# Cross attention: the key tile of 65 keys moves from the eighth to the sixth step of each group

## What is computed

```python
hidden = jnp.concatenate([context, latents], axis=1)      # 1601 + 256 keys
q = (latents @ Wq.T)      # 16 heads of 96
k = (hidden @ Wk.T)       # 4 key heads, each shared by 4 query heads
v = (hidden @ Wv.T)
scores = jnp.einsum('bkgqd,bksd->bkgqs', q, k) * scale
attn = jax.nn.softmax(scores, axis=-1)
out = jnp.einsum('bkgqs,bksd->bkgqd', attn, v)
return out @ Wo.T
```

## Time and profile before

| what | value |
|---|---|
| median of 3 runs | 1926.09 us (1922.92 to 1926.54) |
| profiled execution, its own time | 1923.49 us |
| its span, first to last instruction | 1921.7 us |
| TensorE busy with matmuls | 1871.0 us, 97% |
| VectorE busy | 1233.9 us, 64% |
| ScalarE busy | 1175.2 us, 61% |
| GpSimd busy | 681.4 us, 35% |

### The profile page before, as it was taken

How to read it: one execution, slowest core, us unless ns; L and a number is a source line. 1 busy time by engine, 2 the same in 40 slices (tenths; PEclk the granted TensorE clock), 3 DMA queues, 4 the chain that set the end, 5 groups by cost and what they waited for, 6 DMA issues and landing times. The chain is left out here.

```text
span 1921.7 us, 28060 instructions
## 1 busy us (share of the span) xinstructions
PE 1871.0 (97%) x9512; PEld 1538.3 (80%) x9512; DVE 1233.9 (64%) x2123; ACT 1175.2 (61%) x2067; POOL 681.4 (35%) x696
## 2 busy tenths in 40 slices
PE   7999999999999999999999999999999999999798
PEld 5888888888888788877779877788777797777576
DVE  5656656566566712578865688745788656887654
ACT  6666656666566633467775577764677755777620
POOL 5666757667576522112103012121121030110331
PEclk9999999999999999999999999999999999999899
DMA  4000101001010354200102001111001023000220
GB/s 171 28 28 28 49 15 45 27 27 44 11 55 13 114 193 128 56 5 17 28 20 72 19 9 28 28 39 56 5 17 28 20 72 139 9 17 9 90 83 28
DMA packets 59577, 89.86 MB, mean 47 GB/s; under 512 B 7252, under 2 KB 42452, under 8 KB 58710
## 3 DMA queue, kind: packets, MB, share of 16 engines
q1 hardware_dynamic: 59480, 88.57, 14.6%
HBM read 67.52 MB, written 21.03 MB: 46 GB/s over the span
## 5 line engine op out<-in xcount | busy, mean ns | idle before, releaser
L1152 PE MATMUL b_o_ps<-b_pr,b_v 128*97 128x512 f32 (+1 forms) x1440 | 376.1, 394 | 5.0 <-DVE b_pr L999 4.2
L1139 PE MATMUL b_s<-b_q,b_kt 97*128 97x512 f32 (+1 forms) x1440 | 374.6, 394 | 0.0
L1260 DVE TENSOR_REDUCE b_mx<-b_m 128x1 f32<-128x1024 f32 (+1 forms) x256 | 286.8, 1120 | 110.4 <-PE b_m L1110 109.6
L999 DVE TENSOR_TENSOR b_pr<-b_pf,b_pr 128x1024 fp32r<-128x1024 f32 (+1 forms) x256 | 314.6, 1229 | 65.3 <-ACT b_pr L993 65.1
L1211 ACT ACTIVATE b_pf<-b_s 128x1024 f32<-128x1024 f32 (+1 forms) x256 | 247.9, 968 | 127.9 <-PE b_s L1139 127.3
L1152 PEld LDWEIGHTS b_o_ps<-b_pr,b_v 128*97 128x97 f32 (+1 forms) x1440 | 232.1, 162 | 103.9 <-issue 12.2
L1308 POOL TENSOR_TENSOR b_y<-b_recs,b_o 96x512 f32<-96x512 f32 x32 | 41.3, 1291 | 769.1 <-ACT b_recs L1226 769.1
L1139 PEld LDWEIGHTS b_s<-b_q,b_kt 97*128 97x128 f32 (+1 forms) x1440 | 262.8, 185 | 61.8 <-issue 0.8
L993 ACT ACTIVATE b_pr<-b_pf 128x1024 fp32r<-128x1024 f32 (+1 forms) x256 | 257.7, 1007 | 48.3 <-PE b_o_ps L1152 44.6
L445 PE MATMUL a_ring<-a_xt,w_a 128*128 128x512 f32 x1128 | 276.8, 396 | 0.0
L445 PEld LDWEIGHTS a_ring<-a_xt,w_a 128*128 128x128 f32 x1128 | 207.2, 189 | 40.5
(11 more groups left out here) (119 smaller groups left out, 2594.4 us busy)
## 6 DMA issues: line engine op xcount, KB each, us to landing
hraw<-in_ctx_t SPq DMA_DIRECT2D x92, 128.0 KB, 2.4
raw_a<-in_w_qkv SPq DMA_DIRECT2D x30, 384.0 KB, 3.3
raw_a<-in_w_o SPq DMA_DIRECT2D x32, 256.0 KB, 3.1
queries<-a_q SPq DMA_DIRECT2D x24, 256.0 KB, 2.0
b_qraw<-queries SPq DMA_DIRECT2D x16, 384.0 KB, 3.9
attended<-b_y SPq DMA_DIRECT2D x32, 192.0 KB, 2.1
c_yraw<-attended SPq DMA_DIRECT2D x3, 1536.0 KB, 7.0
x_t<-a_xt SPq DMA_DIRECT2D x2, 2048.0 KB, 8.3
```

What stands on the lines that cost most here:

```text
L999: dve.tensor_tensor(pr[0:rows, k % 2, LO, 0:n], pf[0:rows, k % 2, 0:n], f(pr[0:rows, k % 2, HI, 0:n]), ALU.subtract).then_inc(p_lo.sem, 1)
L1139: mm = pe.matmul(ps_s[k % 2][0:rows, i * BANK:(i + 1) * BANK], kt[:, a, kv, t0:t0 + rows], q[:, kv % 2, m, hp * BANK:(hp + 1) * BANK], sta ...
L1152: mm = pe.matmul(ps_o[0:HD2 + 1, :], v[0:rows, a, t, g // 2, :], pr[0:rows, k % 2, m, i * BANK:(i + 1) * BANK], start=t == 0 and s == 0, s ...
L1260: dve.reduce_max(mx[:, g % 2, t, half:half + 1], ps_m[:, 0:MAXW[half][1]], X).then_inc(mx_made.sem, 1)
```

## The change

The tiles of a step come from a table. Steps 0 to 4 keep their pairs, step 5 takes tile 14 alone, and steps 6 and 7 take the pairs 10, 11 and 12, 13. The accumulation over the group begins and ends with the first and last matmul of the new order. The number of instructions stays the same; what is scheduled at which step j stays too.

```diff
-PAIRS = (NT2 + 1) // 2
+TILES_OF_STEP = [[2 * j, 2 * j + 1] for j in range(5)] + [[NT2 - 1], [10, 11], [12, 13]]
+PAIRS = len(TILES_OF_STEP)
...
-            j = k % PAIRS
-            return [(i, 2 * j + i) for i in range(2) if 2 * j + i < NT2]
+            return list(enumerate(TILES_OF_STEP[k % PAIRS]))
...
-                                       start=t == 0 and s == 0, stop=t == NT2 - 1 and s == 2)
+                                       start=(j, i, s) == (0, 0, 0), stop=(j, i, s) == (PAIRS - 1, len(keys_of(k)) - 1, 2))
```

## The result

The changed kernel takes 1934.05 us (median of 7 runs, 1929.34 to 1937.58); the kernel before, run beside it, 1926.09 us (7 runs, 1922.92 to 1928.44). The ratio is 1.004, with a 95% interval from 1.0025 to 1.0054: **slower by 8 us, where 1933 us and +8.4 us were forecast**.

What follows compares the result with a forecast made beforehand. TensorE sets the pace, with no idle entry in a group. Terms 9.6 - 2.35 - 0.4 + 1.5 = +8.4 us, from the 1924.8 us centre of the times, gave 1933 us; the range was 1927 to 1939.

Steps and rivals of the forecast that it cites:

- Term 1: At `pv(3)` in groups 1 to 6: a new wait, 0.35 us of delay, 0.40 us a group, 24 times, +9.6 us.
- Term 2: At `pv(6)`, ends of group 1 and the last batch's group 3: 5 waits of 0.47 us go, -2.35 us.
- rival (d): Low parts of steps 7 and 6 meet GpSimd and come late: +4 to +8 us more, 1937 to 1941; chance 0.17.
- Terms 3 and 4: Group 7's `pv(0)` wait for the copied output goes, -0.4 us; last batch's end, now a full step, net +1.5 us.
- (a): At `pv(3)`: the wait is absorbed by TensorE or an earlier VectorE chain; sum -1.3 us, 1923.5 us; chance 0.14.
- (b): At `pv(3)`: the wait is half, 0.15 to 0.2 us; +3 to +4 us, 1928.5 us; chance 0.13.
- (c): Low part of step 6 starts ahead of GpSimd in all 11 places, VectorE's chain earlier: 1920.7 us; chance 0.04.
- "in place": Before term 1's wait, the light runs take back 0.69 us, so the row ending a group stands where it stood.

## Why the prediction was right, term by term

**Term 1, the wait at pv(3).** Forecast 0.35 us of delay and 0.40 us a group in 24 groups. In group 1 `pv(3)` stands 857.12 - 856.05 = 1.07 us after scores that need 0.70 and then takes 1.61 us where 1.56 was usual: 0.37 + 0.05. This wait was right in its place, its cause and its size. Groups 1 and 3 are 25.02 (864.18 - 839.16) and 24.99 us long in batch 0 where they were 24.53 and 24.54. 24 x 0.42 = 10.1 us against 9.6. That it is the sums' chain, and the cover behind the maximum, is shown by the four positions that the tile was put in (2, 3, 5 and 6) and by moving the sums alone.

**Term 2, waits that go.** End of group 1 with the change:

```profile
863.44 1.22 DVE L999 TENSOR_TENSOR b_pr<-b_pf,b_pr 128x1024 fp32r<-128x1024 f32 x1
...
863.78 1.77 POOL L1315 CAST b_q<-b_qraw 96x1024 fp32r<-96x1024 f32 x1 [5.25 <-PE b_s L1139]
864.18 0.40 PE L1121 MATMUL b_x<-b_idr,b_neg 128*1 128x128 f32 x4
...
864.94 1.58 PE L1152 MATMUL b_o_ps<-b_pr,b_v 128*97 128x512 f32 x6
...
866.43 2.68 DVE L999 TENSOR_TENSOR b_pr<-b_pf,b_pr 128x1024 fp32r<-128x1024 f32 x1
...
869.60 1.56 PE L1152 MATMUL b_o_ps<-b_pr,b_v 128*97 128x512 f32 x6
```

The roles are exchanged: the low part came first and took 1.22 us, and GpSimd's cast, 1.03 us before, took 1.77. `pv(6)` follows the row by 0.76 us instead of 1.17. The Trainium skill's page "SBUF — State Buffer", section "Who interferes with whom", says that of a VectorE instruction with two SBUF inputs and a GpSimd instruction that reads SBUF the first to issue holds the shared ports and the other is blocked; both orders in these rows agree: the one that came second took 1.77 us. The full low part of step 7 took 2.68 us behind GpSimd and ended at 869.11, 0.49 us early: rival (d) had its lengthening, not its wait.

The 6 ends of groups where GpSimd has context, which I put at 0, gave something too. The end of group 3:

```profile
910.50 0.67 DVE L999 TENSOR_TENSOR b_pr<-b_pf,b_pr 65x512 fp32r<-65x512 f32 x1
...
910.62 3.24 POOL L1301 TENSOR_TENSOR a_hid<-hraw,a_hid 128x256 fp32r<-128x256 f32 x4
...
913.46 1.48 DVE L999 TENSOR_TENSOR b_pr<-b_pf,b_pr 128x1024 fp32r<-128x1024 f32 x1
```

The low part of step 5 that blocks GpSimd's first piece is the short one now, so the four pieces take 3.24 us instead of 3.79, and the low part of step 6 is held for 0.26 us instead of 0.6. The move shortened an instruction that I had on my list and did not follow to the engine it blocks. `pv(6)` stands 0.89 to 0.91 us after its row in these 6 places, where it was 1.16 to 1.19 before: some 0.3 us each. (The bound of +0.7 us that I gave for them was too high by its own words: a piece of 0.95 us less the 0.60 that the low part met is 0.35.)

**Terms 3 and 4, group 7 and the end.** Together +1.4 us were forecast for the last batch; from its last row to its last value matmul it is 26.45 instead of 24.90 us, +1.55. The wait for the copied output is gone, as said, and the last six matmuls stand alone behind 0.79 us of idle. The kernel with the old order in group 7 takes 1.25 us of it back.

**What was missed.** The sum left out that group 0 has no light `pv(7)` of a group before it: its row comes 0.7 us sooner (23.24 instead of 23.95 us), in 4 batches, -2.9 us. The joins at the end of batches 0 to 2 give it back. A join held three light runs before (`pv(7)` of group 6, the scores and `pv(7)` of group 7) and holds two with the change (scores and `pv` of step 5 of group 7). By that count each should be 0.7 us longer, 2.1 us in all, where I had put nothing for `pv(7)`, on the ground that projections cover it, and -0.1 for the rest. They are 1.3, 0.5 and 0.8 us longer, +2.6 us; since joins differ by as much between kernels that share their order there, the count is argued and not shown by an experiment. What failed is the cover: it hides a late input, but a full run in place of a light one still takes TensorE's own time. That the two omissions nearly cancel is luck of structure and not my argument, which had said "in place" for every group. In all: groups 1 to 6 +6.5 us (forecast 7.25), group 0 -2.9, joins +2.6, last end +1.55: +7.8 us for the stretch.

**The rivals.** (a) falls: `pv(3)` waits, and in the rows above nothing is made good behind it. The isolated gap of 216 ns a matmul from the Trainium skill's page "TensorE: Matmul & The Clock Gate", section "Back-to-back issue gap", is not reached: six in a run take 1.39 us, 232 ns each. Behind the wait they take 1.44 us (857.12 to 858.56), since the first takes 0.28. Weight loads fill 80% of the span, and still no time is made good. (b) falls: groups 1, 3 and 5 lose 0.38 to 0.48 us each. (c) had its place right, and waits beside GpSimd did go, but VectorE's chain still hangs on the maximum, as its idle entry of 0.83 us shows.

## What to carry to other kernels

Where the engine that sets the pace is never idle, count instructions last: look up how early each of its inputs is, and which chain makes it. Taking work from between a chain's start and its use has the same effect as making the chain longer, so the cheap step of a loop belongs where no long chain is under way, here ahead of the maximum that starts the sums or behind the `pv(3)` that ends the chain. When a short instruction moves, follow it also to the engine that it blocks, and settle the first and the last round of the loop by themselves.

## What the runs showed of the hardware

A wait in a stream of matmuls costs more than its idle time: idle 0.21 us at `pv(3)` is 0.37 us of delay from start to start, since no matmul drains beside the next there, and the six matmuls after it take 1.60 us instead of 1.55. From the end of VectorE's low part to the first matmul that it releases it was 0.14 to 0.15 us at every wait that the profile puts down to a low part; at `pv(0)` of the kernel with the later split of queries it was 0.10 us (866.68 to 866.78). The granted clock early in the kernel differs between executions of the same self attention: at 42 to 46 us it was 0.50 in one and 1.00 in another. These two reached the cross attention 5.3 us apart, 3.0 of it from that stretch, where the change itself is worth 7.8 us of the stretch behind it.
